# A two-layer graph attention kernel: ScalarE's third cast of a step is put behind the next step's first exponential

## The reference

```python
def transformer_conv(x, src, dst, Wq, bq, Wk, bk, Wv, bv, Ws, bs, H, C, concat):
    n = x.shape[0]
    q = (x @ Wq + bq).reshape(n, H, C)
    k = (x @ Wk + bk).reshape(n, H, C)
    v = (x @ Wv + bv).reshape(n, H, C)
    alpha = jnp.einsum('ehc,ehc->eh', q[dst], k[src]) / jnp.sqrt(jnp.float32(C))
    amax = jax.ops.segment_max(alpha, dst, num_segments=n)
    p = jnp.exp(alpha - amax[dst])
    denom = jax.ops.segment_sum(p, dst, num_segments=n) + 1e-16
    out = jax.ops.segment_sum(p[:, :, None] * v[src], dst, num_segments=n)
    out = out / denom[:, :, None]
    out = out.reshape(n, H * C) if concat else out.mean(axis=1)
    return out + x @ Ws + bs

h = jax.nn.relu(transformer_conv(x, ..., 4, 128, True))
x = _layernorm(x + transformer_conv(h, ..., 2, 128, False), axis=-1)
```

## Time and profile before

| | |
|---|---|
| median of 3 runs | 1960.0 us (1957.96 to 1960.8) |
| the profiled execution: time, span | 1960.0 us, 1957.8 us |
| TensorE (PE) busy | 1813.7 us, 93% of the span |
| VectorE (DVE) busy | 1540.9 us, 79% |
| ScalarE (ACT) busy | 1258.3 us, 64% |
| GpSimd (POOL) busy | 1142.0 us, 58% |
| TensorE's mean granted clock | 0.970 of full speed |
| attention of layer 1, about | 270 to 1245 us |
| attention of layer 2, about | 1430 to 1955 us |

### The profile page before, as it was taken

The page is one execution under the profiler, slowest core; times in us unless marked ns, Lnnn a source line. Parts: engine busy times, 40 slices in busy tenths (PEclk is TensorE's granted clock), DMA queues, the critical chain, the costliest instruction groups (busy, mean ns, idle before and its releaser), DMA issues. The chain is left out here.

```text
span 1957.8 us, 44657 instructions
## 1 busy us (share of the span) xinstructions
PE 1813.7 (93%) x14891; PEld 1350.4 (69%) x14891; DVE 1540.9 (79%) x4569; ACT 1258.3 (64%) x2081; POOL 1142.0 (58%) x1458
## 2 busy tenths in 40 slices
PE   2789969999999999999999999859799999999997
PEld 2555537777777777777777777636467777777776
DVE  5899857888888888888888888522588888888886
ACT  2477647777777777777777777612166666766665
POOL 4000016777767777777677777601267767767775
PEclk9799979999999999999999999979899999999999
DMA  6588766778878877787788878570289999998995
GB/s 143 134 203 204 182 161 129 152 156 157 155 151 157 158 154 152 154 161 154 149 156 160 156 149 148 107 216 1 64 153 170 182 177 167 182 185 174 179 178 108
DMA packets 771276, 302.46 MB, mean 154 GB/s; under 512 B 657124, under 2 KB 751056, under 8 KB 767799
## 3 DMA queue, kind: packets, MB, share of 16 engines
q1 hardware_dynamic: 767143, 295.60, 75.3%
q10 hardware_dynamic: 3266, 2.36, 0.5%
q0 software_dynamic: 640, 1.63, 0.3%
HBM read 93.75 MB, written 48.45 MB: 73 GB/s over the span
## 5 line engine op out<-in xcount | busy, mean ns | idle before, releaser
L1300 DVE CUSTOM_DVE_ANT_0 prob_l<-score_l,mask_l 125x512 f32<-125x512 f32 (+2 forms) x1050 | 644.1, 616 | 215.8 <-PE score_l L1447 214.0
L1447 PE MATMUL score_l<-KT,QT_l 128*128 128x512 f16 (+2 forms) x3150 | 772.1, 355 | 13.0 <-DVE piece_max_l L1300 12.7
L1151 POOL TENSOR_TENSOR prob_parts_l<-prob_l,prob_parts_l 125x512 f16<-125x512 f32 x600 | 721.8, 1233 | 16.0 <-ACT prob_parts_l L1230 16.0
L1221 ACT ACTIVATE prob_l<-prob_l,neg_max_l 125x1024 f32<-125x1024 f32 (+1 forms) x450 | 521.6, 1161 | 4.4 <-DVE neg_max_l L1308 4.3
L1236 ACT CAST probT_l<-transposed_l 128x375 f16<-128x375 f32 x450 | 212.9, 473 | 430.4 <-PE transposed_l L1472 430.4
L1478 PE MATMUL output_l<-V,prob_flipped_l 128*128 128x256 f16 x2400 | 459.5, 272 | 2.9 <-DMA prob_flipped_l<-prob_parts_l 2.9
L1480 PE MATMUL output_l<-V,prob_flipped_l 128*128 128x128 f16 x2400 | 427.4, 219 | 0.0
L1447 PEld LDWEIGHTS score_l<-KT,QT_l 128*128 128x128 f16 x3150 | 282.6, 99 | 144.9 <-DVE piece_max_l L1300 18.8
L1139 POOL CAST QT_l<-q_now_l 128x125 f16<-128x125 f32 x150 | 43.6, 290 | 541.3 <-ACT q_now_l L1208 541.3
L1230 ACT CAST prob_parts_l<-prob_l 125x1024 f16<-125x1024 f32 x300 | 309.5, 1033 | 0.1
L1286 DVE SCALAR_TENSOR_TENSOR mask_l<-mask_l 125x512 f32<-125x512 f32 (+2 forms) x350 | 277.1, 795 | 7.7 <-DMA mask_l<-mask_scratch 7.7
(11 more groups left out here) (170 smaller groups left out, 2023.1 us busy)
## 6 DMA issues: line engine op xcount, KB each, us to landing
mask_scratch<-log SPq DMA_DIRECT2D x79, 448.0 KB
mask_l<-mask_scratch SPq DMA_DIRECT2D x50, 448.0 KB
mask_l<-mask_scratch SPq DMA_DIRECT2D x24, 896.0 KB
mask_l<-mask_scratch SPq DMA_DIRECT2D x24, 471.2 KB
prob_flipped_l<-prob_parts_l SPq DMA_TRANSPOSE x600, 3.3
mask_l<-mask_scratch SPq DMA_DIRECT2D x24, 336.0 KB
hT_scratch<-rowsT_l SPq DMA_DIRECT2D x25, 250.0 KB, 3.7
hT<-hT_scratch SPq DMA_DIRECT2D x6, 1024.0 KB, 14.0
```

What stands on the lines that cost most here:

```text
L1151: pool.tensor_tensor(parts[0:TP, 1, a:b], prob[:, h % 2, a:b], parts[0:TP, 0, a:b], ALU.subtract).then_inc(s_flo, 1)
L1221: act.activation(e, e, ACT.Exp, bias=neg_max[:, h % 2:h % 2 + 1], accum_out=total[:, h % 2, c:c + 1]).then_inc(s_exp, 1)
L1300: dve.tensor_tensor_reduce(out=prob[:, h % 2, a:b], in0=score_bank(h, p)[0:TP, 0:b - a], in1=mask[:, parity, a:b], scale=1.0, scalar=-3.0e ...
L1447: last = pe.matmul(score_bank(h, p)[:, 0:b - a], QT[:, h % 2, i, :], KT[:, h, j, a:b], start=n == 0, stop=n == len(products) - 1)
```

## The change

On ScalarE, in each step, the third cast `high_part(s, h, 2)` is moved from ahead of the exponential part 0 of step s+1 to behind it. Nothing else is added, removed or moved; the instructions, their sizes and their waits stay as they are.

```diff
@@ def tile(t, i, parity), of the ScalarE program in attention()
                     for h in range(H):
                         s = t * H + h
                         tn, hn = ahead(t, h, 1)
-                        for q in range(NQ):
+                        for q in range(NQ - 1):
                             high_part(s, h, q)
                         if exists(tn):
                             exponentials(s + 1, hn, 0)
+                        high_part(s, h, NQ - 1)
+                        if exists(tn):
                             exponentials(s + 1, hn, 1)
                             part_hi(s + 1, hn, 0)
                         if exists(ahead(t, h, 3)[0]):
```

## The result

The changed kernel took 1984.05 us (median of 4 runs, 1982.02 to 1986.21), the kernel before 1960.4 us beside it: a ratio of 1.0126 with a 95% interval from 1.0113 to 1.0137. It is 23.65 us slower, where 18.9 was forecast, inside the range of 1967 to 1988.

What follows compares the result with a forecast made beforehand. TensorE was taken to set the pace of both layers. 25 x (0.33 + 0.01) + 24 x (0.38 + 0.01) + 24 x 0.04 = 18.9 us on 1960.0 gave 1979 us, 8-in-10 range 1967 to 1988.

Steps and rivals of the forecast that it cites:

- Nothing to win from an earlier exponential: ScalarE: exponential part 0 gains up to 0.32 us, spent in the same queue because the next consumer is behind part 1.
- The chain of 2.29 us to the weight load: Layer 1: `neg_max` end, exponential, third cast, `low_part`, weight load of `values` 2; TensorE waits 0.33 us in head 1.
- The sign given for it: Layer 1 profile: weight load of `values` waits for `low_part` about 50 times more than 45, some 17 us more.
- 0.38 in head 3: Layer 1: TensorE waits 0.30 us for late `neg_max`, plus 0.08 as `clear_mask` waits out a later GpSimd instruction.
- A late weight load costs only its lateness: TensorE: a load beginning when its product is due costs nothing measurable, a later one its lateness; 0.01 us taken on top.
- VectorE's 0.64 us are absorbed: Layer 1, head 1: `low_part` 2 and everything behind it come 0.64 us later, hidden by idle time and the later score piece.
- The relu, 0.04 us per tile: Layer 1, head 0: ScalarE's relu ends 0.04 us later and delays TensorE's skip product, 24 times.
- Layer 2 costs 0 to 1 us: Layer 2: `values` 2 keeps 0.28 us of cover after GpSimd's knock-on (0.04 + 0.20); 0 taken, upper bound 1 us.
- it is hidden: Rival: new waits take the place of TensorE's existing ones, time within 4 us of 1960; chance 0.07.
- faster: Rival: the relu chain shortens, idle time before the skip product goes, 7 us won, 1953 us; chance 0.05.
- the slip: Rival: head 3's clear goes ahead of GpSimd's instruction, its 0.38 us wait vanishes, 9.5 us cost, 1969.5 us; chance 0.16.
- more than counted: Rival: full 0.10 weight load, VectorE's lateness at score banks, layer 2's 1 us; at most 29.3, likelier 1984 us; chance 0.14.

Runs made afterwards that it cites:

- the heads 0 and 2 experiment: New order of the cast in heads 0 and 2 of layer 1 alone, against the old-order kernel with plain DMAs for transposing ones: 1959.48 us, 1.6 more.

## Why the prediction was right, and where it was off

- **Nothing to win from an earlier exponential.** Right. ScalarE idles 1.13 us for `neg_max` in head 1, and exponential part 1 starts 0.36 later there; no head got shorter.
- **The chain of 2.29 us to the weight load, with 0.33 in head 1 and 0 in heads 0 and 2.** Right: 2.28, 0.34 by the period, 0.04 (the relu's) and 0.00. The experiments that put the new order into two heads at a time, and the one that moved the skip term, show the cause. The sign given for it was off: the weight load was to wait about 50 times more and some 17 us more, and waited 90 times and 41 us more, since the loads of heads 0 and 2 idle as well, at no cost.
- **0.38 in head 3, with the knock-on through the clear.** Right in the median, 0.39, and the knock-on is shown twice: without the late head 2 the growth is 0.30, without the clear 0. But in 6 of 24 tiles (every fourth, from 0) head 3 did not grow. In those head 2 ahead of it took 9.7 to 9.9 us, where TensorE waited for a flip; the kernel before has that in 3 of them. With the plain DMA neither occurs. So head 3 cost 6.8 us where 9.4 was forecast, and head 2 cost 1.8 where nothing was; heads 0 and 1 cost 0.9 and 8.8 for 1.0 and 8.5. The 18.2 of layer 1 is near the 18.9 partly because these two misses go opposite ways.
- **A late weight load costs only its lateness.** Right: at 745.24 load and product start together, and the period grows by 0.34 for 0.33.
- **VectorE's 0.64 us are absorbed.** Right in layer 1: in head 0 by the heads 0 and 2 experiment, in head 1 by a period that grew by the load's lateness alone.
- **The relu, 0.04 us per tile.** Right: the period of head 0 grew by 0.04, and with the relu moved ahead the idle time before the skip product is gone.
- **Layer 2 costs 0 to 1 us.** Wrong, the mis-sized term: it cost 5.4. The step that failed is "With the knock-on on GpSimd (0.04 + 0.20) 0.28 us of cover are left": it was sized at 0.24 and measured 0.38, and only `values` 2 was held against it. The cover of `values` 2 was enough indeed. The consumer with the least cover was another, `value_sum`, which stands behind the same clear on VectorE and for which `values` 0 waits; it had about 0.2 us to spare and needed 0.38. It makes 22 x 0.19 = 4.2 us of the 5.4. Of the other 1.2 the largest piece is head 1 of tile 13, 11.35 us for 10.04. VectorE had no idle time to take up lateness there: it also does a part of the final layer norm in that step and was busy for 9.94 of the 10.04 us before, against 405.00 of 473.40 over the layer; after, TensorE's transposes wait 0.7 us for its low part. That this is the cause was not tested.

Of the rivals, "it is hidden" and "faster" are refuted by the periods, the slip did not occur (0.11 us of the margin of 0.20 was left), and "more than counted" named 1984 us, which was measured, but by luck: its terms for the weight load and the score banks did not occur, and layer 2's cost came by another way than its own.

## What to carry to other kernels

An instruction that is put behind a wait in an in-order queue costs nothing while its consumer has cover, and then its full lateness; so count for each step the distance from the event waited for to the first use by the engine that bounds the kernel, and hold it against that use's undisturbed time. Where an engine comes later and another shares a port with it, follow the collision to every consumer behind it, not only to the one on the way so far. The start-to-start distance of a repeated instruction shows losses of hundredths of a microsecond that idle times beside modelled ends hide.

## What the runs showed of the hardware that was not expected

A 0.29 us cast on GpSimd took 0.77 us behind a VectorE instruction with two SBUF inputs that began 0.07 us ahead of it and took 0.69, and the low parts behind it then held up the next such instruction on VectorE (1.57 us for 512 columns; the same instruction takes 0.68 where GpSimd is idle, in head 1 of layer 1): one late start grew from 0.24 to 0.38 us in the first of these meetings, and the second passed it on. Plain DMAs in place of the 600 transposing ones changed the time by 0.1% only, although they land after 2.3 us in place of 3.3 and the mean busy share of the DMA engines over layer 1 fell from 0.81 to 0.46.
